# Three moves in a fused two-layer program: products ahead of the inverse roots, unread products around the last quantising turn, and the turned tokens copied first

## What is computed

```python
# layer 0: attention's entry
u = silu(((q - mean(q)) / sqrt(var(q) + EPS) * ln_g + ln_b) @ Wu.T + bu)   # and v, base alike
# layer 0: quantised network; act_qdq takes one scale from the largest absolute value of the whole tensor
x = act_qdq(x)
up, gate = act_qdq(x @ dq(w_up).T), act_qdq(x @ dq(w_gate).T)
gate = act_qdq(gate * fixed_qdq_u16(sigmoid(gate)))
o = act_qdq(gate * up)
y = o @ dq(w_down).T
# layer 1: mixture attention over 16 experts, for each of 2048 tokens
q, k, v = (einsum('ne,neh->nh', w, einsum('nc,ech->neh', x, p)) for p in (q_proj, k_proj, v_proj))
o = softmax(q @ k.T / sqrt(128)) @ v
out = einsum('enh,ehc->nc', einsum('ne,nh->enh', w, o), o_proj)
```

## Time and profile before

| | |
|---|---|
| median of 3 runs | 502.7 us (502.55 to 507.95) |
| profiled execution, its own time | 499.7 us |
| its span, first to last instruction | 497.9 us |
| TensorE busy | 439.2 us, 88% |
| VectorE busy | 405.6 us, 81% |
| ScalarE busy | 234.3 us, 47% |
| GpSimd busy | 54.3 us, 11% |
| mean granted TensorE clock | 0.959 of full |

### The profile page before, as it was taken

One profiled execution on the slowest core, in us unless ns is written; L12 is line 12 of the kernel. 1 busy time (PEld: TensorE's weight loads), 2 busy tenths in 40 slices (PEclk: granted clock), 3 DMA queues, 4 the chain that ended last, 5 costly groups with the idle time before them and its releaser, 6 DMA issues.

```text
span 497.9 us, 9483 instructions
## 1 busy us (share of the span) xinstructions
PE 439.2 (88%) x3709; PEld 308.7 (62%) x3709; DVE 405.6 (81%) x906; ACT 234.3 (47%) x426; POOL 54.3 (11%) x69
## 2 busy tenths in 40 slices
PE   7999899998799989400599999999999999999997
PEld 6446899987348854100289986666656555666676
DVE  6997689877597759999834589996898999899686
ACT  5975555473662229895544554437224322422110
POOL 2014000000580004500082000000000000000000
PEclk9999999999999999855699998999999999999999
DMA  8977997960171003403330007364773000000000
GB/s 276 339 294 323 391 390 307 370 253 1 43 229 68 1 0 115 140 0 126 127 96 0 2 4 254 115 226 155 261 269 96 6 13 7 7 5 7 7 7 26
DMA packets 23474, 66.69 MB, mean 134 GB/s; under 512 B 2979, under 2 KB 5414, under 8 KB 23302
## 3 DMA queue, kind: packets, MB, share of 16 engines
q1 hardware_dynamic: 22992, 65.98, 36.7%
q10 hardware_dynamic: 438, 0.11, 0.1%
HBM read 38.68 MB, written 1.18 MB: 80 GB/s over the span
## 4 chain that ended last, share of the span: by engine, by line
PE 35%; DVE 17%; issue 3%; ACT 1%; DVEq 0%
PE bk L726 12%; PE bk L734 6%; PE bk L771 5%; DVE RA L1694 2%; DVE X L1654 2%; DVE XT L1666 2%; PE bk L608 2%; PE bk L654 2%; DVE RA L1486 1%; DVE WK L1520 1%; PE bk L758 1%; PE bk L746 1%; PE bk L624 1%; DVE QS L1394 1%; PE bk L645 1%
## 5 line engine op out<-in xcount | busy, mean ns | idle before, releaser
L726 PE MATMUL bk<-X,RB 128*128 128x512 f16 x384 | 94.1, 381 | 0.0
L1014 ACT ACTIVATE X<-RA 128x512 f16<-128x512 f32 x64 | 40.2, 630 | 100.5 <-DVE RA L1694 84.4
L1666 DVE SCALAR_TENSOR_TENSOR XT<-bk,WK,XT 128x128 f32<-128x128 f32 x192 | 67.0, 349 | 6.0 <-PE bk L771 0.8
L726 PEld LDWEIGHTS bk<-X,RB 128*128 128x128 f16 x384 | 37.1, 98 | 41.7 <-issue 1.1
L734 PEld LDWEIGHTS bk<-RB,X 128*128 128x128 f16 x768 | 48.3, 98 | 15.1
L734 PE MATMUL bk<-RB,X 128*128 128x128 f16 x768 | 53.3, 219 | 0.0
L1654 DVE TENSOR_TENSOR X<-RA,X 128x512 f16<-128x512 f32 x64 | 43.8, 684 | 1.1 <-ACT X L1014 1.1
L867 ACT ACTIVATE WK<-bk 128x512 f32<-128x512 f32 x48 | 28.5, 594 | 28.8 <-PE bk L404 23.9
L771 PE MATMUL bk<-RB,RA 128*128 128x512 f16 x144 | 38.7, 379 | 0.0
L1301 DVE SCALAR_TENSOR_TENSOR RB<-WK,WCOL,bk 128x512 f32<-128x512 f32 x32 | 23.7, 743 | 12.7 <-ACT WK L867 12.7
L577 PE MATMUL bk<-PK1T,QS 128*128 128x128 f32 x5 | 2.1, 413 | 35.5 <-DVE QS L1397 35.5
(11 more groups left out here) (323 smaller groups left out, 888.5 us busy)
## 6 DMA issues: line engine op xcount, KB each, us to landing
RC<-RA SPq DMA_DIRECT2D x20, 768.0 KB, 5.1
STG<-RA SPq DMA_DIRECT2D x8, 768.0 KB, 5.2
RC<-expert_weights SPq DMA_DIRECT2D x22, 256.0 KB, 6.1
RC<-in_wx SPq DMA_DIRECT2D x7, 768.0 KB, 8.1
X<-in_w SPq DMA_DIRECT2D x8, 512.0 KB, 3.6
RA<-RA SPq DMA_DIRECT2D x4, 768.0 KB, 5.0
RC<-in_w SPq DMA_DIRECT2D x8, 384.0 KB, 4.2
STG<-expert_weights SPq DMA_DIRECT2D x12, 256.0 KB, 6.1
```

The costliest lines, as they stand in the source:

```text
L726: t = e.matmul(BK[m][:, :], P16[:, wp, wo:wo + 128], ZH[:, n % 4, xp, :], start=(e1 == 0 and i == 0), stop=(e1 == 15 and i == 2))
L1014: e.activation(ZH[:, r, 0, :], zf[r], ACT.Copy).then_inc(S("z_hi"), 1)
L1666: stt(XT[:, bb_(t_)], bank_o(n)[:, bb_(i)], RW[:, t_, e1:e1 + 1], XT[:, bb_(t_)], ALU.mult, ALU.add).then_inc(S("acc"), 1)
```

## The change

Three edits. TensorE's entry of attention has `weff(3)` and the `u0` products of columns 0 and 1 ahead of the two root products. In the quantising stage eight matmuls that nobody reads stand ahead of turn 4, behind a wait for the third maximum (`o_max` 3), and six more behind turn 4. In ScalarE's steps the copy of the turned tokens stands ahead of the step's `z_hi`.

```diff
@@ TensorE, entry of attention
             project("base", 1)
             weff(2)
+            weff(3)
+            project("u0", 0)
+            project("u0", 1)
             q.wait_ge("cent", 4)
             rstd(2, BK[0])
             q.wait_ge("var", 4)
             rstd(3, BK[1])
-            weff(3)
-            for name in ("u0", "u1"):
-                for c in range(2):
-                    project(name, c)
+            for c in range(2):
+                project("u1", c)
             for name in ("base", "u0", "u1"):
                 for c in (2, 3):
                     project(name, c)
@@ TensorE, quantising stage
-            for i in range(1, 5):
+            for i in range(1, 4):
                 quant_turn(i)
+            q.wait_ge("o_max", 3)
+            for _ in range(8):
+                e.matmul(BK[6][:, :], FW16[:, 0, 0, :], FW16[:, 0, 0:4, :], start=True, stop=True)
+            quant_turn(4)
+            for _ in range(6):
+                e.matmul(BK[6][:, :], FW16[:, 0, 0, :], FW16[:, 0, 0:4, :], start=True, stop=True)
@@ ScalarE, expert steps
             for k in range(STEPS):
+                if k - 1 in attention and attention[k - 1][1] == 3:
+                    c = attention[k - 1][0]
+                    q.wait_ge("xtmm", c + 1)
+                    e.activation(XT[:, cc(c)], BK[5][:, :], ACT.Copy).then_inc(S("turned"), 1)
                 if 2 <= k < NI:
                     z_hi(k)
...
-                    elif i == 3:
-                        q.wait_ge("xtmm", c + 1)
-                        e.activation(XT[:, cc(c)], BK[5][:, :], ACT.Copy).then_inc(S("turned"), 1)
```

## The result

The changed kernel took 495.96 us in the median of 4 runs (493.75 to 497.28), the kernel before 502.62 beside it. The ratio is 0.9887, 95% interval 0.9858 to 0.9916: 1.1% faster, some 2 us beyond the 498.2 that was forecast and inside its range. The profiled execution took 493.75 us with a span of 492.0, against 499.7 and 497.9.

What follows compares the result with a forecast made beforehand. TensorE, or VectorE where TensorE waits for it, was taken to bound the kernel. 2.1 + 1.3 + 1.1 = 4.5 us off the 502.7 us median gave 498.2 us, range 494.8 to 501.8.

Steps and rivals of the forecast that it cites:

- Part 1: Entry of attention: `weff(3)` and `u0` products fill TensorE's 2.72 us wait ahead of the roots; -2.1 us.
- the gap in part 2: Quantising stage: 1.4 us between the eight unread products and the turn; the clock was taken to stay up.
- Part 2: Quantising stage: fourteen unread products lift the clock before the 36 down products; -1.3 us.
- theory A: Set up for the follow-up runs: three gains simply add, 2.0 + 1.4 + 0.9 us, the first no more than 2.0.
- The median's 3.0 us above the profile: Whole kernel: median 502.7 us, 3.0 above the profiled execution; unexplained, carried over unchanged into the forecast.
- larger: Rival: all 2.2 us of part 3 arrive, or later clock makes part 2 worth 2 to 2.5; 496.9 us, chance 0.25.
- The full price: Quantising stage: all 1.3 us counted, because the eight unread products are 3.4 us dense.
- Part 3: Last third: copying turned tokens earlier removes two TensorE waits of 1.10 us; -1.1 us, bounds 0.4 and 2.2.
- the two new waits: Last third: TensorE would wait 0.4 us for `ot_lo`, and for ScalarE's bank copy at the change of columns.
- Part 1 swallowed: Rival: something taken as hidden, such as GpSimd's rotations, eats the entry's gain; 500.3 us, chance 0.08.
- no clock: Rival: the clock doesn't come up in time for the down products, part 2 gives 0; 499.5 us, chance 0.13.
- The slower one: Rival: clock lifted, then taken back in the gap, all 36 down products slow; 505.3 us, chance 0.04.

Runs made afterwards that it cites:

- e1: Kernel before with only `weff(3)` and the `u0` products moved ahead of the roots; 498.4 us, ratio 0.9933.
- e11: Changed kernel with the entry of attention put back in its order of before; 499.1 us, ratio 0.9934 to the kernel before.
- e4: The changed kernel timed once more, nothing altered; 495.39 us, ratio 0.9869 to the kernel before.
- e9: Kernel before plus eight unread products in TensorE's wait ahead of the first spread root; 500.96 us, ratio 0.9998.
- e7: Changed kernel with ScalarE's `ot_hi` copy also ahead of `z_hi`; 494.59 us, ratio 0.986 to the kernel before.
- e8: Changed kernel with ScalarE's `ot_hi` copy and the third column group's query bank copy also ahead of `z_hi`; 493.85 us, ratio 0.9844 to before.
- e3: Kernel before with only ScalarE's copy of the turned tokens moved ahead of `z_hi`; 500.52 us, ratio 0.9962.
- e2: Kernel before with only the fourteen unread products around the last quantising turn; 498.35 us, ratio 0.9926.
- e12: e8 without the eight unread products ahead of the last quantising turn, the six behind it kept; 494.14 us, ratio 0.9853 to before.
- e5: Kernel before with only the eight unread products ahead of the last quantising turn; 501.54 us, ratio 1.0017.
- e6: Kernel before with only the six unread products behind the last quantising turn; 500.57 us, ratio 0.9982.
- e10: e8 plus four unread products ahead of the third router's logits; 493.84 us, ratio 0.9845 to the kernel before.

## Why the prediction was right, and where it was short

**Part 1, forecast 2.1.** The moved work gave 1.97 us, by the steps named: the idle time 0.57, the `xn_lo` back to back, the rotation not late. Missing was a term. The prediction took from one row (L471, 1.02 us before and after the wait) that the clock outlasts the 2.72 us, and used it as evidence for the gap in part 2. In that execution it did. In five of the six profiled executions with this entry it did not, and in none of the seven with part 1 is there a fall. By these profiles part 1 is worth 3.4 us on average, 1.4 beyond the moved work, and by the mean clocks about 1.7 beyond it. The times agree: e1 won 3.4 us (1.9 to 4.8), and the ratios of e11 and e4 are 0.0065 apart, 3.3 us with an uncertainty of some 1.9. Neither excludes the 2.0 of theory A by itself, and e9, which fills the wait and moves nothing, shows the clock but no gain in time. So the fall and what it costs where it occurs are shown; that filling the wait wins this time in the timed runs is likely, and rests on these sums.

**The median's 3.0 us above the profile.** "No row tells why. I carry the difference over": this is the step that failed. It was no constant. The profiled execution had no further low stretch, like 10 of the 66 other runs of this kernel. An average run has 1.48 of them, at 1.6 us each 2.4 of the 3.0; the clocks of the three runs behind the 502.7 are not on record. The spread of the runs does not tell the kernels apart: e4's six lie within 0.8 us, the changed kernel's four and e1's nine within 3.5, and e11's eleven, without part 1, within 1.9. So the forecast for the profiled execution was good (4.5, measured 4.1), and the one for the median 2 us short. 4.1 + 1.7 = 5.8 us, where the two comparisons measured 5.7 (4.2 to 7.1) and 6.6 (5.1 to 8.0). With the same 1.7 us the rows of the table make 6.9 for e7 and 7.3 for e8, where 7.0 (5.7 to 8.4) and 7.8 (6.6 to 9.1) were measured. The rival "larger" had the right suspicion, the clock in the timed executions, and put it into part 2. Most of it was at the entry, but not all: the down products of e1, e3 and e9 take 0.2 to 0.7 us longer than those of before, so the profiled execution was a good one there too. Averaged over the profiles of before, e1, e3 and e9, part 2 wins 1.6 us from B to C and not 1.4. e2's timed runs won 3.7 us (2.3 to 5.1), and why they won so much stays open.

**Part 2, forecast 1.3.** 1.4 from B to C; the start of L624 follows VectorE as worked out. Not foreseen was that 0.2 to 0.5 us go again before D, in every kernel whose down products were sped up in full (133.0 to 133.25 instead of 132.75). e12, whose profile has no low stretch near 300 us, gives nothing back (132.81). The low stretch near 300 us then falls further into the products of the last third: in the changed kernel the first six take 2.74 us, where they took 2.23 before. Why it lies elsewhere stays open. The full price was right, but its reason (the eight, 3.4 us dense) was not: e5's profile shows them worthless alone, and e6's the six sufficient.

**Part 3, forecast 1.1.** 1.0, with the two new waits as named, 0.47 and 0.23 us. But the first was described as a limit of VectorE, and the row quoted for it said something else: VectorE's `ot_lo` itself waited 0.58 us for ScalarE (L1062), behind the same `z_hi`. Read to its end, that row gives e7 and e8, and with both copies moved 2.6 us, more than the upper bound of 2.2. That the rest is VectorE's own standing of twice 0.58 us is argued, not shown.

**The rivals.** "Part 1 swallowed" and "no clock" did not occur. The slower one is real as a mechanism (e5), but it needs the six away, and then costs nothing measurable.

## What to carry to other kernels

Before one profiled execution is taken for the timed ones, set its mean granted clock beside that of the other runs: steps of the same size are low stretches, and work that fills a wait of TensorE may win them back on top of the wait itself. When a wait is removed, follow what is late next through every engine's own wait: the row that names VectorE's result may carry ScalarE in its brackets. Where unread products are to hold the clock, they belong right ahead of the work that needs it.

## What the runs showed of the hardware that was not expected

One program, run again, gets a different number of low stretches: 0 to 4 beyond the usual ones in 66 runs of the kernel before, each 3.4 us long where a profile shows it and, over those runs, worth 1.6 us on average. The same wait of 2.72 us was followed by one in the profiled executions of e2, e3, e5, e6 and e11 and by none in that of before. Eight dense products were followed by the high level in e5, and it was gone again after 2.63 us of standing; with six more in between, it held through a gap of 1.33 us (the changed kernel). But the same eight left the clock low in e2, e10 and e11, where the turn behind them took 0.47 us and not 0.32; there it came up only behind the six. And a low stretch needs no long standing ahead of it: in the changed kernel the granted clock is 1.00 from 290 to 295 us, 0.89 from 295 to 296 and 0.50 from 296 to 298, and from 290 to 296 us the rows show TensorE busy for 5.89 us of 6, mostly with small float32 products.
